# A fifth scaled product: in three tiles out of four, ACT and POOL take one expert's product from DVE in the MoE layers of a fused transformer block

## What is computed

```python
probs = jax.nn.softmax(x @ Wg, axis=-1)              # 8 experts
top_vals, top_idx = jax.lax.top_k(probs, 2)
gates = top_vals / jnp.sum(top_vals, axis=-1, keepdims=True)
expert_out = jnp.einsum('th,ehd->etd', x, We) + be[:, None, :]
out = jnp.sum(gates[..., None] * expert_out[top_idx, tok, :], axis=1)
x = x + 0.5 * out
```

## Time and profile before

| | |
|---|---|
| median of 3 runs | 467.35 us (465.76 to 472.85) |
| the profiled execution, own time | 468.03 us |
| its span, first to last instruction | 465.9 us |
| PE busy in the span | 404.1 us, 87% |
| DVE busy | 362.4 us, 78% |
| ACT busy | 278.5 us, 60% |
| POOL busy | 249.7 us, 54% |
| mean granted clock of PE | 0.978 of full |

### The profile page before, as it was taken

The page is one execution under the profiler, slowest core; times in us unless marked ns, Lnnn a source line. Parts: engine busy times, 40 slices in busy tenths (PEclk is TensorE's granted clock), DMA queues, the critical chain, the costliest instruction groups (busy, mean ns, idle before and its releaser), DMA issues.

```text
span 465.9 us, 11688 instructions
## 1 busy us (share of the span) xinstructions
PE 404.1 (87%) x3280; PEld 287.6 (62%) x3296; DVE 362.4 (78%) x1284; ACT 278.5 (60%) x758; POOL 249.7 (54%) x431
## 2 busy tenths in 40 slices
PE   0778888775799999999999999999998898888884
PEld 0656666553466666666667666766765676666652
DVE  3989999986877786686677678677666458999995
ACT  4666777352275566657566566655656567667753
POOL 8976666543245544544554454454445435676654
PEclk9999999887999999999999999999999899999998
DMA  3311000035644354344535535443540000001001
GB/s 112 92 56 22 0 1 0 1 100 148 171 118 152 117 155 116 111 139 111 149 102 147 134 102 149 113 147 108 152 130 9 6 1 1 25 24 45 23 23 45
DMA packets 45792, 39.11 MB, mean 84 GB/s; under 512 B 5896, under 2 KB 42524, under 8 KB 45754
## 3 DMA queue, kind: packets, MB, share of 16 engines
q1 hardware_dynamic: 43706, 38.14, 29.0%
q10 hardware_dynamic: 2048, 0.53, 0.6%
HBM read 22.61 MB, written 15.20 MB: 81 GB/s over the span
## 4 chain that ended last, share of the span: by engine, by line
PE 43%; POOL 22%; issue 14%; ACT 8%; DVE 5%; DMA 2%; ACTq 2%; SPq 2%; POOLq 1%; DVEq 0%
PE bank L916 10%; POOL m_pair L217 9%; PE bank L901 8%; PE bank L886 6%; ACT a_weights L733 5%; POOL m_upper L221 4%; PE bank L889 4%; PE bank L881 4%; POOL m_rstd L229 3%; PE bank L997 2%; PE bank L1008 2%; ACTq L725 2%; PE bank L1011 2%; DVE a_neg_max L794 1%; DMA x_all<-in_L_attn_x 1%
## 5 line engine op out<-in xcount | busy, mean ns | idle before, releaser
L794 DVE TENSOR_REDUCE a_neg_max<-bank 128x2 f32<-128x512 f32 (+1 forms) x192 | 123.7, 685 | 62.6 <-PE bank L889 59.9
L673 POOL TENSOR_SCALAR_AFFINE_SELECT a_weights<-a_weights 128x512 f32<-128x512 f32 (+1 forms) x96 | 75.5, 787 | 108.7 <-ACT a_weights L733 104.0
L733 ACT ACTIVATE a_weights<-bank 128x512 f32<-128x512 f32 x192 | 107.0, 591 | 35.0 <-issue 22.0
L251 ACT ACTIVATE m_scaled<-bank,m_gates 128x128 f32<-128x128 f32 x256 | 72.3, 365 | 26.2 <-PE bank L417 26.2
L901 PE MATMUL bank<-a_q_rows,a_k_rows 106*128 106x512 f32 (+1 forms) x192 | 73.7, 451 | 4.9 <-ACT a_weights L733 4.9
L217 POOL TENSOR_TENSOR m_pair<-m_scaled 128x256 f32<-128x256 f32 x64 | 47.5, 742 | 50.8 <-ACT m_scaled L251 50.7
L294 DVE SCALAR_TENSOR_TENSOR m_lower<-bank,m_gates,m_lower 128x128 f32<-128x128 f32 x192 | 66.0, 344 | 2.3 <-issue 0.2
L886 PE MATMUL bank<-a_k_rows,a_q_rows 104*128 104x256 f32 x256 | 59.3, 335 | 0.4 <-DVE a_neg_max L794 0.4
L889 PE MATMUL bank<-a_mask,a_ident 128*128 128x256 bf16 (+1 forms) x176 | 56.2, 320 | 0.0
L916 PE MATMUL bank<-a_weights,a_v 128*32 128x128 f32 x1536 | 52.7, 279 | 0.0
L886 PEld LDWEIGHTS bank<-a_k_rows,a_q_rows 104*128 104x128 f32 x256 | 40.6, 194 | 14.5 <-DVE a_neg_max L794 10.1
(11 more groups left out here) (128 smaller groups left out, 828.5 us busy)
## 6 DMA issues: line engine op xcount, KB each, us to landing
a_k_rows<-k_stage SPq DMA_DIRECT2D x16, 416.0 KB
k_stage<-a_k_parts SPq DMA_DIRECT2D x48, 128.0 KB, 1.8
q_stage<-a_q_parts SPq DMA_DIRECT2D x48, 128.0 KB, 1.9
a_q_rows<-q_stage SPq DMA_DIRECT2D x64, 96.0 KB
a_k_heads<-k_stage SPq DMA_DIRECT2D x64, 52.0 KB
a_q_dense<-q_stage SPq DMA_DIRECT2D x16, 192.0 KB
x_all<-in_L_attn_x SPq DMA_DIRECT2D x8, 256.0 KB, 2.8
out_x<-x_all SPq DMA_DIRECT2D x8, 256.0 KB, 2.3
```

What stands on the lines that cost most here:

```text
L251: last = nc.scalar.activation(scaled[:, q % 2, j], y_high[q % 2][:, j * D:(j + 1) * D], ACT.Copy, scale=gates[:, s % 2, q, 4 + j:5 + j])
L673: nc.gpsimd.affine_select(out=diagonal, in_=diagonal, compare_op=ALU.is_ge, fill=0.0, base=0, pattern=[[0, heads.stop - heads.start], [1, P]],
L733: nc.scalar.activation(weights[n // 2][:, half:half + 4, :].rearrange("p h n -> p (h n)"), wt_bank[n % 2][:, :], ACT.Exp).then_inc(wt_exp, 1)
L794: nc.vector.tensor_reduce(neg_max[:, t, heads], score_bank[p % 2][:, :].rearrange("p (h n) -> p h n", n=(t + 1) * P), AX.X, ALU.max, negat ...
```

## The change

`scaled` gets a fifth slot per buffer. In the tiles q0, q2 and q3 (`low_of(q) == 3`) DVE issues e0 to e2 only. ACT issues a fifth scaled product, of expert 3 from `y_low`, behind its four; it waits until DVE's e2 of the same tile is done. `high_used` now comes with the fifth. POOL issues a third add in these tiles, between the pair add and the upper sum: the fifth slot onto the first half of the pair sum. In q1 all is as before. The counts of the semaphores `low_chain` (13 per group where there were 16) and `pair_done` (7 where there were 4) follow.

```diff
-    scaled = sb("scaled", [P, 2, 4, D], FP32)
+    scaled = sb("scaled", [P, 2, 5, D], FP32)
...
+    low_of = lambda q: 4 if q == 1 else 3
+    low_count = lambda i, q: i * 13 + (0, 3, 7, 10)[q]
+    pair_count = lambda i, q: i * 7 + (0, 2, 3, 5)[q]
+    tile_ahead = lambda i, q: (i, q - 1) if q else (i - 1, 3)
...
-            pool.wait_ge(pair_done, t + 1)
+            pool.wait_ge(pair_done, pair_count(i, q) + 1)
+            if low_of(q) == 3:
+                nc.gpsimd.tensor_tensor(pair[:, q % 2, 0], pair[:, q % 2, 0], scaled[:, q % 2, 4],
+                                        ALU.add).then_inc(pair_done, 1)
+                pool.wait_ge(pair_done, pair_count(i, q) + 2)
...
-            at_least(act, pair_done, t - 1)
+            if not (s == 0 and q < 2):
+                act.wait_ge(pair_done, pair_count(*tile_ahead(i, q)))
...
+            if low_of(q) == 3:
+                act.wait_ge(low_chain, low_count(i, q) + 3)
+                last = nc.scalar.activation(scaled[:, q % 2, 4], y_low[q % 2][:, 3 * D:4 * D], ACT.Copy,
+                                            scale=gates[:, s % 2, q, 3:4])
             last.then_inc(high_used, 1)
...
-            dve.wait_ge(low_chain, t * 4 + 4)
-            nc.vector.tensor_tensor(tile(t), lower[:, q % 2, 3], upper[:, q % 2], ALU.add).then_inc(upper_used, 1)
+            dve.wait_ge(low_chain, low_count(i, q) + low_of(q))
+            nc.vector.tensor_tensor(tile(t), lower[:, q % 2, low_of(q) - 1], upper[:, q % 2], ALU.add).then_inc(upper_used, 1)
...
-            if B:
+            if B and low_of(q) == 4:
                 expert(i, s, q, 3)
...
-            at_least(pe, low_chain, (t - 1) * 4)
+            if not (s == 0 and q < 2):
+                pe.wait_ge(low_chain, low_count(*tile_ahead(i, q)))
```

More of the change, by code:

```diff
@@ L292, in expert @@
             else:
-                dve.wait_ge(low_chain, t * 4 + j)
+                dve.wait_ge(low_chain, low_count(i, q) + j)
             nc.vector.scalar_tensor_tensor(out=lower[:, q % 2, j], in0=y_low[q % 2][:, j * D:(j + 1) * D],
@@ L297, in expert, with finish @@
                                            op0=ALU.mult, op1=ALU.add).then_inc(low_chain, 1)
-        def finish(t, q):
+        def finish(i, q):
+            t = i * Q + q
             dve.wait_ge(upper_done, t + 1)
-            dve.wait_ge(low_chain, t * 4 + 4)
-            nc.vector.tensor_tensor(tile(t), lower[:, q % 2, 3], upper[:, q % 2], ALU.add).then_inc(upper_used, 1)
+            dve.wait_ge(low_chain, low_count(i, q) + low_of(q))
+            nc.vector.tensor_tensor(tile(t), lower[:, q % 2, low_of(q) - 1], upper[:, q % 2], ALU.add).then_inc(upper_used, 1)
         def after_link(n, k):
@@ L392, in part @@
             if B and not (s == 0 and q == 0):
-                finish(i * Q + q - 1, (q - 1) % 2)
+                finish(*tile_ahead(i, q))
             if q == 2 and A:
@@ L403, in part @@
             if q == 3 and s == G - 1:
-                finish(G * Q - 1, 1)
+                finish(i, 3)
         return part
```

## The result

| | before | after |
|---|---|---|
| median | 467.29 us (465.76 to 472.85) | 515.38 us (508.58 to 517.51) |
| profiled execution, own time | 468.03 | 514.29 |
| its span | 465.9 | 512.2 |
| mean granted clock | 0.978 | 0.946 |

The medians are 48 us apart. An execution over 1.5% above the fastest of its kernel counts as slow, and ratios are taken from the others, here 508.58 and 514.29 (the traces of experiments 5 and 9 are of slow ones). The forecast of 504.5 had the sign and most of the size; the median lies at the upper end of the range (516). From here on `finish` is L319, the bias added is L360, `expert` L309, the fifth product L266, the pair add, the third add and the upper sum L223, L227 and L231, and `xn` L290.

The account below looks back on a forecast made before the run. DVE was taken to set the MoE pace, 9.73 us per group. Ten full groups at 3.1 us (31) plus 6 for three partial ones made 37 on 468.03, 505; against the median 504.5 us, range 490 to 516.

Parts of the forecast that it names:

- The chain behind e2 of q0: From e2 of q0 over ACT's fifth product and POOL's adds: `rstd_of` at 2.75, `xn` 4.92, `finish` of q2 9.75.
- The loop: e2 of q0 to the next over ACT, POOL, DVE: period 12.32 against 9.73; as rival without collision 499 us, chance 0.25.
- The collision: `finish` of q2 on DVE held under POOL's pair add of q3: about 0.53 us per group, period 12.85.
- The step that failed: PE's clock in the MoE groups: no fall expected at 70% busy, since 72% from 10 to 22 us kept 1.00.
- the rival: PE's clock falls: bias bank at 11.8 instead of 10.5, 1 to 2 us more per group, 515 to 525; chance 0.09.
- the forecast's case: MoE groups with the loop and the collision, PE's clock not falling: period 12.85, 504.5 us; chance 0.50.
- Beside the groups: The groups beside attention, between the MoE layers, wait for other things: 0 us added.
- The three ends: First group of each layer and last of the second: 2 us each, 6 us in all.
- the bias bank with 0.2 us in hand: PE's q0 matmuls fill the bias bank at 10.5, against 10.73 where DVE wants it; hidden by q2's `finish`.

Follow-up runs that it names:

- experiment 5: Changed kernel without POOL's third add, expert 3's product left out of the sum in q0, q2 and q3: 494.6 us, ratio 1.055.
- experiment 9: Kernel before with expert 3's product moved in q1 only, made first by ACT ahead of DVE's e0: 473.85 us, ratio 1.012.
- experiment 2: Changed kernel with POOL's pair add of q3 waiting until DVE's `finish` of q2 is done: 508.56 us, ratio 1.087.
- experiment 3: Changed kernel with both the idle matmuls of experiment 1 and the added POOL wait of experiment 2: 501.66 us, ratio 1.075.
- experiment 4: Changed kernel with `rstd_of` on POOL moved ahead of the adds of q0: 491.51 us, ratio 1.055.
- experiment 7: Changed kernel cut to the fifth product in q0 only: 499.37 us, ratio 1.072.
- experiment 8: Kernel before with expert 3's product moved in q0 and q1, made first by ACT, DVE's e0 waiting for it: 472.83 us, ratio 1.015.
- experiment 1: Changed kernel with seven idle matmuls per full group on PE, into a bank nobody reads: 505.73 us, ratio 1.083.
- experiment 6: Changed kernel cut to the fifth product in q2 and q3 only: 477.2 us, ratio 1.023.
- experiment 11: Control: kernel before with three idle matmuls per full group on PE: 468.38 us, ratio 1.003.
- experiment 10: Kernel of experiment 9 with three idle matmuls per full group on PE: 472.56 us, ratio 1.015.
- experiment 12: Kernel of experiment 10 with POOL's pair adds of q1 and q3 waiting for DVE's gap and q2's `finish`: 469.4 us, ratio 1.002.

## Why the prediction was right, and where it fell short

- **The chain behind e2 of q0** held to a tenth: `rstd_of` at 2.82 (forecast 2.75), `xn` at 4.84 (4.92), `finish` of q2 at 9.77 (9.75). That the last is so close is partly luck: the third add costs its queue 0.61 in q0 (64.98 to 65.59) where I took 0.54, from `rstd_of` to `xn` it is 2.02 where I took 2.17, and from the end of q2's upper sum to `finish` 0.12 (72.96 to 73.08) where I took 0.03.
- **The loop** was sized right: 12.39 to 12.45 with neither the collision nor the low clock (experiments 2 and 3), against 12.32. Experiments 4, 7 and 8 show its links one by one: move `rstd_of`, 18 us less; q0 alone, 34 us; q0 with the same work but no wait for e2, 7 us, q1's product included. Ten such groups were to make 31 us and made 36.6; with the clock full they make 30.2 (experiment 1).
- **The collision** was right in place and price: `finish` 0.73 under a pair add, period 12.82 with it and 12.43 without, so 0.4 of the forecast's 0.53. The forecast's period with the collision, 12.85, is what the changed kernel does at the full clock. In the changed kernel itself it is mostly hidden by the late bank.
- **The step that failed** is "From 10 to 22 us it was busy 8.60 of 12, 72%, and the granted clock stayed at 1.00, the level of 2.4 GHz, so I expect no fall". One stretch of that busy share proved nothing for another: the groups of after have PE at 9.91 of 12 in its own, slower time, and the clock fell in most of them and hardly in two. The price in the rival for it was right: the bank full at 11.8, and it is (75.13 against 63.31). What it adds to the period is 0.8 (13.61 against 12.82), not 1 to 2, because the collision had already moved the bias add to 11.3. Experiment 1 is the forecast's case run by itself: 505.7 us against 504.5.
- **Beside the groups** I had 0 for the stretch around attention, and in the two traces compared it is 3.4. No run shows that it is the change's doing. From the last full group of the first layer to the first bias add of the second it is 303.4 us in the kernel before and 306.7 in the changed one; in experiments 1 to 7, each with a part or all of the change, it is 301.8 to 305.7, and in the control of experiment 11, without any, 304.7. So executions differ there by as much. The three ends came to 6.6, against 6.
- **Still open:** whether ACT could take the fifth product while DVE reads the same bank was not tried; what holds experiment 4 at 10.9; and what makes the clock fall in one group and not in the next.

## What to carry to other kernels

Before an instruction is moved to an engine with spare time, write down what it waits for and everything queued behind it there, and follow the path until it meets itself: the length of that closed loop, not the busy share, is the new period. Price the wait and the work apart, since the same product in the same tile cost 34 us behind e2 and 7 us, with another one beside it, when ACT took it first. A wait on one engine also empties the others, and PE pays for that a second time through its clock, so ask what stands second in line, here the bias bank with 0.2 us in hand.

## What the runs showed of the hardware that was not expected

- PE's granted clock fell to 0.50 in the middle of a loop in which the longest idle time before one of its instructions was 1.34 us, and 7 idle matmuls per group (of about 0.24 us each at the full clock) kept it at 1.00 in every full group (experiment 1). Whether it fell differed from group to group in one execution: in the changed kernel, periods of 12.8 and 13.6 stand next to each other.
- Even a small DVE instruction can be held under a POOL add: 128 x 4 numbers took 0.60 where they take 0.15 (experiment 10). But the same instruction under POOL's power, which runs for 1.04 us and reads SBUF too, took its usual 0.15 (experiment 12). The Trainium skill, SBUF — State Buffer, section "SBUF: two separate sides", has the later of the two fully blocked for the whole of the earlier instruction. The DVE instructions under the pair adds, which end 0.02 (the gap) to 0.15 us (`finish`) behind them, agree with it; the one under the power doesn't.
- Such collisions come and go with the phase of the two queues. In the first layer experiment 10 lost 0.65 us per group (10.4 for 9.75), to holds of which the kernel before has two, that of the gap and that of q2's `finish`, in one group each (at 399 and 395 us). In the second layer of the same execution some groups have them and some don't.
